# Two-layer AdaLN/FFN kernel: the residual add of every third swept tile moved from GpSimd to VectorE

## What is computed

```python
def _L1_cond_ref(x, weight, adapter_ids):
    w = weight[adapter_ids]
    return jnp.einsum('bsi,boi->bso', x, w)

def _L1_ffn_ref(input, weight, bias, centroids, assignments):
    x = input.reshape(-1, shape[-1])
    dots = jax.nn.softmax(x @ centroids.T / TEMPERATURE, axis=-1)
    hits = dots > THRESHOLD
    query_sel = jnp.any(hits, axis=1)
    cluster_sel = jnp.any(hits, axis=0)
    row_sel = cluster_sel[assignments]
    dense = x @ weight.T + bias
    return jnp.where(query_sel[:, None] & row_sel[None, :], dense, 0)

x = x + _L0_ffn_ref(_L0_cond_ref(x, ...), ...)
x = x + _L1_ffn_ref(_L1_cond_ref(x, ...), ...)
```

## Time and profile before

| | |
|---|---|
| median of 3 runs | 633.07 us |
| the profiled execution, its own time | 633.0 us |
| its span, first to last instruction | 631.3 us |
| granted TensorE clock, mean | 0.97 |
| busy: PE, DVE, ACT, POOL | 562.3, 423.3, 182.5, 367.9 us |
| the sweep, from GpSimd's first output add to the end of the span | 539.9 to 631.3 us |
| busy in 540 to 632 us: PE, DVE, ACT, POOL | 66.6, 59.7, 11.4, 73.6 us |

### The profile page before, as it was taken

One profiled execution on the slowest core, in us unless ns is written; L12 is line 12 of the kernel. 1 busy time (PEld: TensorE's weight loads), 2 busy tenths in 40 slices (PEclk: granted clock), 3 DMA queues, 4 the chain that ended last, 5 costly groups with the idle time before them and its releaser, 6 DMA issues.

```text
span 631.3 us, 10738 instructions
## 1 busy us (share of the span) xinstructions
PE 562.3 (89%) x3298; PEld 470.9 (75%) x3298; DVE 423.3 (67%) x877; ACT 182.5 (29%) x346; POOL 367.9 (58%) x385
## 2 busy tenths in 40 slices
PE   0899999999999998869999988998899999899780
PEld 0689999999999853646667766787788886678570
DVE  6797667657756784655768755795456668688680
ACT  4443333322222213323333423342221132111110
POOL 5422264765665573464667766976596100688885
PEclk9899999999999999889999999998899999999995
DMA  6977567689887226894677898998896630466631
GB/s 193 204 215 219 157 147 224 169 234 241 247 235 216 85 78 201 258 298 165 228 242 259 266 362 293 357 363 296 295 348 242 200 104 15 146 220 214 238 143 58
DMA packets 91239, 136.87 MB, mean 217 GB/s; under 512 B 29048, under 2 KB 45790, under 8 KB 90162
## 3 DMA queue, kind: packets, MB, share of 16 engines
q1 hardware_dynamic: 75314, 95.08, 51.3%
q0 software_dynamic: 12912, 40.45, 16.5%
q10 hardware_dynamic: 2960, 0.67, 0.6%
HBM read 87.17 MB, written 50.84 MB: 219 GB/s over the span
## 4 chain that ended last, share of the span: by engine, by line
PE 55%; POOL 13%; DMA 12%; DVE 8%; issue 5%; SPq 4%; ACT 1%; POOLq 0%; ACTq 0%; DVEq 0%
PE acc L2076 16%; PE work L2020 9%; PE acc L2302 9%; POOL out_tile L1053 5%; POOL out_dram L1044 5%; PE bcast L2173 3%; DMA x_by_tile<-x_rows 3%; PE bcast L2291 3%; DMA two_rows<-expert_deltas_sorted 2%; PE work L2004 2%; PE work L2243 2%; PE bcast L2134 2%; DMA cond_w<-in_L_cond_weight_dram 2%; PE acc L2207 2%; PE acc L2173 2%
## 5 line engine op out<-in xcount | busy, mean ns | idle before, releaser
L948 POOL TENSOR_TENSOR yT_lo<-y_masked,yT_hi 128x512 fp32r<-128x512 f32 x29 | 38.3, 1322 | 72.7 <-ACT yT_hi L1122 72.6
L1253 ACT ACTIVATE x1T_hi<-work 128x512 fp32r<-128x512 f32 x66 | 39.4, 598 | 139.5 <-PE work L2243 139.0
L985 POOL DMA_INDIRECT gated_by_expert<-records,record_places x64 | 62.8, 981 | 20.2 <-issue 17.2
L1771 DVE TENSOR_TENSOR x1T_lo<-work,x1T_hi 128x512 fp32r<-128x512 f32 x66 | 45.3, 686 | 43.1 <-PE acc L2302 22.0
L1732 DVE TENSOR_TENSOR x_group<-acc,base_b_bc 128x512 f32<-128x512 f32 x79 | 50.3, 682 | 23.4 <-PE acc L2209 23.4
L2020 PE MATMUL work<-uT_hi,hankel 128*128 128x512 f32 (+3 forms) x256 | 64.8, 326 | 0.8 <-DVE y_masked L1505 0.8
L2302 PE MATMUL acc<-merged_w_hi,x1T_hi 128*128 (+1 forms) x156 | 46.0, 417 | 5.4 <-DVE x1T_lo L1771 5.4
L1025 POOL DMA_INDIRECT expert_deltas_sorted<-x_group,two_rows x36 | 35.9, 997 | 22.8 <-DVE x_group L1732 15.8
L2020 PEld LDWEIGHTS work<-uT_hi,hankel 128*128 128x128 f32 x256 | 45.7, 189 | 3.8 <-issue 1.0
L1053 POOL TENSOR_TENSOR out_tile<-out_tile,cond_w 128x512 f32<-128x512 f32 x14 | 18.2, 1301 | 48.9 <-DVE out_tile L1921 48.6
L1025 POOL DMA_INDIRECT expert_deltas_sorted<-x_group,records_of_slots x31 | 30.5, 985 | 26.3 <-DVE x_group L1732 19.0
(11 more groups left out here) (367 smaller groups left out, 1351.2 us busy)
## 6 DMA issues: line engine op xcount, KB each, us to landing
hankel<-k_rev SPq DMA_DIRECT2D x32, 512.0 KB, 6.9
x_group<-in_x_dram SPq DMA_DIRECT2D x32, 256.0 KB, 3.8
cond_w<-in_L_cond_weight_dram SPq DMA_DIRECT2D x28, 256.0 KB, 4.3
x_rows<-x_base_sorted SPq DMA_DIRECT2D x25, 256.0 KB, 5.0
x_by_tile<-x_rows SPq DMA_DIRECT2D x25, 256.0 KB, 4.6
x_rows<-x_by_tile SPq DMA_DIRECT2D x24, 256.0 KB, 3.0
two_rows<-expert_deltas_sorted SPq DMA_DIRECT2D x10, 512.0 KB, 5.6
cond_w<-expert_deltas_sorted SPq DMA_DIRECT2D x9, 512.0 KB, 6.0
```

What stands on the lines that cost most here:

```text
L948: g.tensor_tensor(yT[h % 2][1][:, :, :], y32[h % 2][:, :, :], yT[h % 2][0][:, :, :].bitcast(F32), ALU.subtract).then_inc(y_lo, 1)
L985: g.indirect_dma_start(rec_dram, bass.IndirectOffsetOnAxis(ap=place_u[to][:, m:m + 1], axis=0), both[:, m, :], None, bounds_check=last_pla ...
L1253: a.activation(xts[n % 2][0][:, :, :], wb[n % 2][:, :], ACT.Copy).then_inc(xd_hi, 1)
L1771: v.tensor_tensor(xts[n % 2][1][:, :, :], wb[n % 2][:, :].rearrange("p (k b) -> p k b", k=LB), xts[n % 2][0][:, :, :].bitcast(F32), ALU.su ...
```

## The change

`BY_DVE` names every third swept tile: i = 1, 4, 7, 10, 13, 16, 19 and 22, 8 of 27. For these VectorE masks the tile into the PSUM bank that the kept tiles use and adds the residual rows from there, with the code of the kept tiles; GpSimd then only scatters the tile. These adds are counted on the semaphore `k_rdy` together with those of kept tiles, in the order in which VectorE makes them, and SyncE's loads of the rows of tile i+8 wait on `k_rdy` for them. GpSimd's other 19 tiles are as before.

```diff
+BY_DVE = tuple(i for i in range(NP - 2) if i % 3 == 1)
...
+        dve_made = []
+        for j in range(CHOSEN + 1, NP):
+            dve_made += [SWEPT[i] for i in range(selected_by(j - 1), selected_by(j)) if i in BY_DVE]
+            dve_made += [KEPT_TILES[k] for k in range(kept_out_by(j - 1), kept_out_by(j))]
...
+        def rows_added(eng, i):
+
+            if i in BY_DVE:
+                eng.wait_ge(k_rdy, dve_done(SWEPT[i]))
+            else:
+                eng.wait_ge(o_rdy, pool_done(i))
...
-                        sp.wait_ge(o_rdy, i + 1)
+                        rows_added(sp, i)
                         load_rows(SWEPT[i + RB], rows[i % RB], s_rl[i % RB])
...
-                pool.wait_ge(ft_sel, i + 1)
-                pool.wait_ge(s_rl[n], rows_loaded(i))
-                g.tensor_tensor(outt[n][:, :], outt[n][:, :], rows[n], ALU.add).then_inc(o_rdy, 1)
-                pool.wait_ge(o_rdy, i + 1)
+                if i not in BY_DVE:
+                    pool.wait_ge(ft_sel, pool_done(i))
+                    pool.wait_ge(s_rl[n], rows_loaded(i))
+                    g.tensor_tensor(outt[n][:, :], outt[n][:, :], rows[n], ALU.add).then_inc(o_rdy, 1)
+                rows_added(pool, i)
                 store_out(SWEPT[i], outt[n][:, :], s_out[n])
...
+            def masked_and_added(tile, t, x_rows, loaded, count):
+
+                if dve_done(t) > 1:
+                    dve.wait_ge(k_rdy, dve_done(t) - 1)
+                chain.after(v.scalar_tensor_tensor(masked_kept, tile, query[:, t:t + 1], rowsel_ps,
+                                                   ALU.mult, ALU.mult))
+                dve.wait_ge(loaded, count)
+                v.tensor_tensor(tile, masked_kept, x_rows, ALU.add).then_inc(k_rdy, 1)
+
             def select(i):
 
                 n, t = i % RB, SWEPT[i]
                 dve.wait_ge(ft_sum, i + 1)
+                if i in BY_DVE:
+                    masked_and_added(outt[n][:, :], t, rows[n], s_rl[n], rows_loaded(i))
+                    return
```

More of the change, by code:

```diff
@@ L559, in kept_out_by, with dve_done, pool_done @@
             return 0 if j <= CHOSEN else (j - CHOSEN + 1) // 2 if n <= 0 else min(KEPT, LAG + 2 * (n // 3) + min(n % 3, 2))
+        dve_made = []
+        for j in range(CHOSEN + 1, NP):
+            dve_made += [SWEPT[i] for i in range(selected_by(j - 1), selected_by(j)) if i in BY_DVE]
+            dve_made += [KEPT_TILES[k] for k in range(kept_out_by(j - 1), kept_out_by(j))]
+        def dve_done(t):
+            return dve_made.index(t) + 1
+        def pool_done(i):
+            return sum(u not in BY_DVE for u in range(i + 1))
+        def rows_added(eng, i):
[3 more added lines that the diff above has]
+                eng.wait_ge(o_rdy, pool_done(i))
         def merged(m):
@@ L839, in _ @@
                     if k + 2 < KEPT:
-                        sp.wait_ge(k_rdy, k + 1)
+                        sp.wait_ge(k_rdy, dve_done(KEPT_TILES[k]))
                         load_rows(KEPT_TILES[k + 2], rows_kept[k % 2], s_rk[k % 2])
@@ L1060, in _ @@
                 for k in range(kept_out_by(j - 1), kept_out_by(j)):
-                    pool.wait_ge(k_rdy, k + 1)
+                    pool.wait_ge(k_rdy, dve_done(KEPT_TILES[k]))
                     store_out(KEPT_TILES[k], kept[k][:, :], s_kout)
@@ L1924, in out_of_kept @@
             def out_of_kept(k):
-                t = KEPT_TILES[k]
                 if k == 0:
                     dve.wait_ge(ft_ev, KEPT)
[L1929 to L1934, removed]
+                masked_and_added(kept[k][:, :], KEPT_TILES[k], rows_kept[k % 2], s_rk[k % 2], 16 * (k // 2 + 1))
             for j in range(CHOSEN + 1, NP):
```

## The result

| | before | with the change |
|---|---|---|
| median of 6 runs | 631.79 us | 621.07 us (617.22 to 621.89) |
| ratio, 95% interval | | 0.9846 [0.9814, 0.9879] |
| the profiled execution, its span | 633.0, 631.3 us | 621.89, 620.1 us |
| GpSimd's first output add begins | 539.92 us | 538.25 us |
| GpSimd's last scatter ends | 627.18 us | 616.08 us |

The change makes the kernel 1.5% faster, 9.7 us by the ratio (the medians differ by 10.7 us). The ratio on the 633.07 us from which the forecast was made gives 623.3 us, where 623.5 were forecast. The interval of the ratio is 0.33% either way, where the prediction counted on 0.2%.

The account below looks back on a forecast made before the run. GpSimd's queue from its first output add to its last scatter was taken to set the end; 10.4 us off less 0.9 us of early waits gives 9.5 us, from 633.0 to 623.5 us, range 621.3 to 626.3 us.

Parts of the forecast that it names:

- The bound: Sweep: from its first output add to its last scatter, 87.26 us, GpSimd hardly waits for other engines and sets the end.
- The relief: GpSimd's queue: eight adds go, each tile costing 1.29 instead of 2.59 us, 10.4 us off; all 39 scatters stay.
- The early waits: Start of the sweep: GpSimd meets VectorE at tiles 3 and 4, losing 0.7 and 0.2 us, together 0.9 us.
- the second wait: GpSimd waits for VectorE's add of tile 4, 0.2 to 0.7 us; 0.2 us was taken.
- VectorE's cost: VectorE's sweep: eight masks with add at 1.39 instead of 0.66 us, 5.8 us more, covered by GpSimd's arrears.
- Rival (a): VectorE becomes the bound, keeping 7.2 us of waits for kept rows plus 5.8 us of adds: 629.4 us; chance 0.05.
- Full-length operations: VectorE's sweep: if each operation took its full length, 72 us instead of some 66, ending near 614 us; sum stands.
- The queues: SyncE's row loads come earlier, by up to 9 us; DMA share rises to 0.8 at most; cost taken as nothing.
- rival (b): Kept tiles' rows at steps 16 to 22, crowded out by faster scatters, land later: slower, 636.6 us; chance 0.03.
- The pauses: Three unexplained GpSimd pauses ahead of scatters, 1.9 us; 622.0 us if the two later vanish, 625.0 if as large ones recur.

Follow-up runs that it names:

- kept rows first: Kernel before, with SyncE's loads of kept tiles' rows moved two steps ahead of the swept tiles' loads from step 12 on; ratio 0.9996, stretch 87.37 us.
- the dose: The changed kernel with 4, 11, 18 or 27 swept tiles' adds on VectorE instead of 8; ratios to the kernel before 0.9924, 0.9795, 0.9871, 0.9919.
- loads late: Changed kernel, with SyncE's row loads of tiles 15, 18, 21 and 24 also waiting for GpSimd's next add; ratio to the kernel before 0.9855.
- not added: Kernel before, with no residual rows added to the eight tiles by either engine; ratio 0.9865, stretch 79.24 us.
- added twice: Kernel before, with VectorE masking and adding the eight tiles while GpSimd adds their rows too; ratio 1.0006, stretch 88.48 us.
- thirteen: Changed kernel with thirteen tiles on VectorE, thin early and dense late, and a ninth row buffer; ratio to the kernel before 0.9742, stretch 70.70 us.
- before, ninth buffer: Kernel before, with a ninth row buffer so that tile 8's rows load before the sweep; ratio 1.0005, stretch 87.19 us.

## Why the prediction was right, and where it was thin

- **The bound.** GpSimd's queue alone set the end: shown by kept rows first (VectorE 4.9 us sooner, no gain) and by the dose, 1.24, 1.30 and 1.29 us a tile with 4, 8 and 11 tiles, the waits ahead of tiles 3 and 4 taken off.
- **The relief.** 8 x 1.30 = 10.4 us; with the waits counted the sum meets the measured stretch to 0.01 us. A scatter behind a scatter costs 1.29 us also when it is a swept tile's.
- **The early waits.** A loss of 0.7 and 0.2 us was forecast, waits of 0.75 and 0.23 us were found. Their place and cause were right. The idle time ahead of tile 3's add was called "about 1 us" since the pause of 0.34 us ahead of tile 2's scatter was taken off there; it stayed, and the loss is the same either way. For the second wait the lower end of 0.2 to 0.7 us was chosen, and it fits. Left out was that TensorE's granted clock can be halved behind its idle time there, which makes the first wait 2.4 to 2.6 us in kernels with eight or eleven tiles on VectorE or off GpSimd. The prediction read 1.00 in the rows and took it as given. That the clock didn't fall in the profiled execution of the change was luck; a fall lengthens the stretch by 1.4 us (loads late and "not added"), which would have stayed inside the range.
- **VectorE's cost.** 1.39 us for mask and add, 5.8 us in all, hidden: added twice stayed within 0.35% of the kernel before, and all but 0.1 us of its stretch's 1.2 us is the one wait of 1.15 us. Rival (a) fell because its premise did: the waits for kept rows went from 7.2 to 0.4 us with the arrears. VectorE binds only beyond 11 tiles; with thirteen the last scatters already wait for it.
- **Full-length operations.** The Trainium skill ("VectorE: DVE Perf Modes", "The DRAIN you can't avoid"), the rule taken alone as the prediction weighed it, would put operations 0.69 to 0.75 us apart. The new ones start 0.60 to 0.66 us apart here too, but for an add behind its own mask, 0.78; the trace agrees with the exemption of the page's next section and not with the rule alone.
- **The queues.** The DMA share rose to 0.83 in one stretch of 10 us (0.65 before in the same one), above the 0.8 called the most. From 550 to 600 us the loads into `x_rows` land in 3.3 us at the median (3.1 before), swept tiles' scatters in 3.8 (3.3). So transfers do land later, as rival (b) had it, but by little. The rule of the Trainium skill cited there ("DMA: Bandwidth & Descriptors", "Queues, rings and completion order") would let that happen, and no run here tests it by itself.
- **The pauses.** In the change they neither vanished nor multiplied. What makes them stays open.

## What to carry to other kernels

When one engine's queue is behind its work to the end (in arrears), price its instructions from start to start and take them off: the gain is their number times that, until the next engine is as full, and the idle time that others show meanwhile is worth nothing by itself. Cutting arrears also takes away the cover of every stall upstream, so look for the first place where the relieved engine will meet the one before it, and remove the stall there in the same edit. Compare such edits by a stretch of the trace that begins behind the common part: it told 1 us apart where the times scattered by 4. It is a single execution, so look at the granted clock in it first: a fall alone moved it by 1.4 us.

## What was unexpected of the hardware

- An idle time of TensorE of 2.3 to 2.5 us was followed, in five of the nine profiled executions that had it, by a granted clock of 0.50 for some 3.4 us, beginning a good microsecond after work had resumed. Longer ones occurred twice, later in the sweep: 3.17 us of idle time (added twice) was followed by the same 3.4 us at 0.50, and behind 4.27 us (before, ninth buffer) the clock fell before work had resumed and stayed at 0.50 for 6.8 us.
- GpSimd pauses 0.34, 0.48 and 1.07 us longer than usual ahead of the 4th, the 13th and the 35th scatter of the sweep, to 0.01 us the same in the kernel before and in ten others, though up to eleven adds fewer stand between. In all eleven these are the scatters of swept tiles 2, 9 and 23, each behind GpSimd's own add. With thirteen tiles and the ninth buffer no such pause appears, and there VectorE adds to just these three. With 18 and 27 tiles on VectorE they are mixed with waits for it. The cause was not looked for.
